# First layer's opening in the form of the second's, set-up products one to a slot, and POOL's second weight split one chunk earlier

## The reference, cut to what matters

```python
# layer 0
mod = silu(condition) @ Wada + bada
sh_a, sc_a, gt_a, sh_m, sc_m, gt_m = split(mod, 6)
xm = layernorm(x, g1, be1) * (1 + sc_a) + sh_a
x = x + gt_a * attention(xm)              # causal
xm = layernorm(x, g2, be2) * (1 + sc_m) + sh_m
x = x + gt_m * (gelu(xm @ W1 + b1) @ W2 + b2)
# layer 1: scale and shift from cond @ w_adaln.T + b, key padding mask, no gates
```

## Time and profile before

| | us |
|---|---|
| median of 3 runs | 1145.15 |
| lowest and highest run | 1138.78, 1145.33 |
| profiled execution | 1142.95 |
| its span | 1141.2 |
| TensorE busy | 1077.1 (94%) |
| DVE busy | 787.0 (69%) |

### The profile page before, as it was taken

How to read it: one execution, slowest core, us unless ns; L and a number is a source line. 1 busy time by engine, 2 the same in 40 slices (tenths; PEclk the granted TensorE clock), 3 DMA queues, 4 the chain that set the end, 5 groups by cost and what they waited for, 6 DMA issues and landing times.

```text
span 1141.2 us, 24601 instructions
## 1 busy us (share of the span) xinstructions
PE 1077.1 (94%) x8972; PEld 943.2 (83%) x8972; DVE 787.0 (69%) x2379; ACT 614.0 (54%) x1239; POOL 262.5 (23%) x269
## 2 busy tenths in 40 slices
PE   3869999999999998999998999999999988999998
PEld 3768898988987687899887788888888767988997
DVE  5467888888886566655647778787787755566553
ACT  1146666666665634443433777777777764344431
POOL 5111131221323334223411111211112221121111
PEclk9779999999998999999997999999999988999999
DMA  7656877667671010000058649465574400010001
GB/s 217 102 85 101 121 139 124 116 106 129 150 106 19 7 61 10 10 10 11 14 86 121 87 71 172 63 92 80 78 92 61 58 2 1 20 37 20 19 20 37
DMA packets 50832, 81.52 MB, mean 71 GB/s; under 512 B 8916, under 2 KB 23476, under 8 KB 49620
## 3 DMA queue, kind: packets, MB, share of 16 engines
q1 hardware_dynamic: 50232, 79.16, 40.0%
q10 hardware_dynamic: 480, 0.79, 0.6%
HBM read 22.64 MB, written 8.44 MB: 27 GB/s over the span
## 4 chain that ended last, share of the span: by engine, by line
PE 84%; DVE 5%; DMA 4%; issue 2%; ACT 2%; SPq 2%; ACTq 0%; POOL 0%; POOLq 0%; DVEq 0%
PE g_bank L573 15%; PE st_bank L573 14%; PE o_bank L661 9%; PE o_bank L573 8%; PE s_bank L573 8%; PE s_bank L628 6%; PE st_bank L647 5%; PE st_bank L641 4%; PE s_bank L624 3%; PE st_bank L643 3%; PE g_bank L719 2%; DMA k_stack<-qk_split 2%; SPq L430 1%; PE s_bank L771 1%; PE s_bank L625 1%
## 5 line engine op out<-in xcount | busy, mean ns | idle before, releaser
L860 ACT ACTIVATE probs<-st_bank 128x384 f32<-128x384 f32 (+1 forms) x512 | 274.1, 548 | 146.1 <-PE st_bank L643 82.7
L1154 DVE CUSTOM_DVE_ANT_0 s_bank<-s_bank,tri_wide 128x128 f32<-128x128 f32 (+1 forms) x512 | 170.2, 386 | 35.4 <-PE s_bank L625 34.2
L1160 DVE TENSOR_REDUCE maxima<-s_bank 128x2 f32<-128x512 f32 x256 | 168.3, 684 | 27.9 <-PE s_bank L628 27.3
L952 ACT ACTIVATE probs<-st_bank,cols 128x512 f32<-128x512 f32 x112 | 77.1, 689 | 202.3 <-PE st_bank L573 186.8
L573 PE MATMUL st_bank<-qk_split,q_stack 128*128 128x512 f32 x696 | 168.4, 400 | 4.9 <-ACT probs L952 4.0
L573 PEld LDWEIGHTS st_bank<-qk_split,q_stack 128*128 128x128 f32 x696 | 130.4, 190 | 37.7 <-ACT probs L952 5.4
L573 PE MATMUL g_bank<-xmT,wa 128*128 128x256 f32 x768 | 122.3, 299 | 4.8 <-POOL xmT L1355 4.8
L661 PE MATMUL o_bank<-probs,v_sb 128*32 128x256 f32 (+1 forms) x2048 | 125.7, 364 | 0.0
L628 PE MATMUL s_bank<-k_stack,q_stack 97*128 97x256 f32 x512 | 116.1, 312 | 6.5 <-DMA k_stack<-qk_split 2.7
L1355 POOL TENSOR_TENSOR xmT<-xm_full,xmT 128x512 fp32r<-128x512 f32 x32 | 42.3, 1322 | 321.4 <-ACT xmT L926 321.4
L573 PEld LDWEIGHTS g_bank<-xmT,wa 128*128 128x128 f32 x768 | 105.1, 200 | 5.8 <-issue 5.2
(11 more groups left out here) (121 smaller groups left out, 2143.4 us busy)
## 6 DMA issues: line engine op xcount, KB each, us to landing
q_stack<-qk_split SPq DMA_DIRECT2D x192, 128.0 KB, 4.6
k_stack<-qk_split SPq DMA_DIRECT2D x186, 128.0 KB, 6.1
gate_rows<-gate_dram SPq DMA_DIRECT2D x32, 128.0 KB, 3.4
w_dram<-w_in SPq DMA_DIRECT2D x8, 512.0 KB, 7.1
wm_f32r<-w_dram SPq DMA_DIRECT2D x4, 1024.0 KB, 10.1
out<-x_sb SPq DMA_DIRECT2D x8, 512.0 KB, 2.9
x_sb<-x_in SPq DMA_DIRECT2D x4, 512.0 KB, 7.0
q_stack<-q_stack SPq DMA_DIRECT2D x4, 384.0 KB
```

The costliest lines, as they stand in the source:

```text
L860: activation(probs[:, h % 8, 0:n], st_bank[h % 2][:, 0:n], ACT.Exp, scale=SCALE)\
L952: activation(h_of[b.const > 0][:, m % 2], h_bank(b, m)[:, :], ACT.Gelu, bias=cols[:, cb + m:cb + m + 1]).then_inc(m_gelu, 1)
L1154: last = v.tensor_tensor_reduce(out=bank[:, keys], in0=bank[:, keys], in1=tri_wide[:, T - (i + 1) * P:T], scale=1.0, scalar=LOWEST, op0=AL ...
L1160: v.reduce_max(maxima[:, gb.mod(2), :, slot], bank[:].rearrange("p (i n) -> p i n", n=T), AX.X).then_inc(max_done, 1)
```

## The change

Five things move.

1. The calls ahead of layer 0's loop are now new(0), project(0), new(1), project(1), on PE and ACT, and the loop starts at step 2 without a projection of q and k, as in layer 1. The v projection of batch 1 stays in slots 6 and 7 of step 2 (`v_due`). On DVE only project(0) stands ahead of the loop; its low parts of batch 1 stay in step 2 among the maxima of batch 0. The six DMAs of k for batch 1 are issued by ACT as those of batch 0 are.
2. `set_up(s)` replaces `set_up_columns` and `set_up_rows` on PE: slots 0 to 11 hold one pair of L539's instructions each, slots 12 and 13 two row instructions each, slot 14 the two for the bias. It writes to o_bank instead of s_bank. It is called for layer 0 in any `step` whose t is AHEAD, and that is so for two calls: `step(0, Step(2), "project")` ahead of the loop, and step 2 in the loop.
3. DVE's part of the set-up stands behind step 2 instead of ahead of it.
4. SyncE's `store_tables` and `load_gates` stand behind the two restacks of a step instead of ahead of them; `load_x(2)` stands behind the restack of q of batch 1.
5. POOL's split of the second attention weights stands in `mlp_step` 2, behind the deviation of chunk 2, instead of in `mlp_step` 3. The memset of the ones columns in v_sb is in two parts.

```diff
+        def v_due(layer, t, only):
+            if layer == 0 and t.const == AHEAD:
+                return only is None
+            return active(layer, t, only)[1].within(B)
...
-            if layer == 1 and t.const == AHEAD:
+            if t.const == AHEAD:
                 return n, off, b, c, d
...
-                    if layer == 0:
-                        when(x_added, c.count(1, -1))
-                        load_gates(c, 0)
...
+                if layer == 0 and c.within(B):
+                    if c.const == 0:
+                        store_tables()
+                    when(x_added, c.count(1, -1))
+                    load_gates(c, 0)
...
+            def set_up(s):
+
+                if s == 0:
+                    pe.wait_ge(late_loaded, 16 * LATE_LOADS)
+                if s < 2 * NF:
+                    last = columns(o_bank, s, ada0, COLUMN_PARTS[2] * D + s * P, silu)
+                elif s < 6 * NF:
+                    last = columns(o_bank, s, ada1, (s - 2 * NF) * P, cond)
...
+                    if layer == 0 and t.const == AHEAD:
+                        set_up(s)
...
+            step(0, Step(0), "new")
+            pe.wait_ge(setup_done, 1)
+            step(0, Step(1), "project")
+            step(0, Step(1), "new")
+            step(0, Step(2), "project")
             for layer in range(LAYERS):
-                for t in steps(B, AHEAD * layer, 5):
...
+                for t in steps(B, AHEAD, 5):
                     step(layer, t)
-                    if layer == 0 and t.const == 1:
-                        set_up_columns()
-                        set_up_rows()
...
-                    if s == SLOT["k"][1] and a.within(B) and a.const + layer == 0:
+                    if s == SLOT["k"][1] and a.within(B) and layer == 0 and a.const < 2:
                         act.wait_ge(k_lo, ga.count(1, 1))
...
+                if layer == 0 and t.const == AHEAD:
+                    a = t - 1
...
-                if layer == 0 and t.const == 3:
+                if layer == 0 and t.const == 2:
                     for f in range(NF):
                         pool.wait_ge(wa_high, 2 + f)
```

More of the change, by code:

```diff
@@ L701, in step @@
                                 last.then_inc(ready, 1)
-                    if s in SLOT["v"] and a.within(B):
+                    if s in SLOT["v"] and v_due(layer, t, only):
                         i = SLOT["v"].index(s)
+                        ga = in_layer(layer, t - 1)
                         if i == 0:
@@ L993, in mlp_step @@
                     step(1, Step(2), "project")
+            step(0, Step(0), "new")
+            step(0, Step(1), "project")
+            step(0, Step(1), "new")
+            step(0, Step(2), "project")
             for layer in range(LAYERS):
-                for t in steps(B, AHEAD * layer, 5):
+                for t in steps(B, AHEAD, 5):
                     if t.const == 3:
-                        act.wait_ge(setup_done, 3)
-                        act.wait_ge(mask_stored, 16)
                         wait(act, m_added, 2 * NCH * layer or None)
@@ L1303, in _ @@
             for layer in range(LAYERS):
-                for t in steps(B, layer + 1, 5):
-                    if layer == 0 and t.const == 1:
-                        split_attention_weights()
+                if layer == 0:
+                    split_attention_weights()
+                    row_statistics(0, Step(1))
+                    row_normalise(0, Step(1))
+                    step(0, Step(1), "project")
+                    set_up_constants()
+                for t in steps(B, AHEAD, 5):
                     step(layer, t)
-                    if layer == 0 and t.const == 1:
+                    if layer == 0 and t.const == AHEAD:
                         set_up_columns()
@@ L1356, in modulated_low, with step @@
                     .then_inc(xmT_ready, 1)
-            def step(layer, t):
-                n, d = t, t - 4
+            def step(layer, t, only=None):
+                n, a, b, c, d = active(layer, t, only)
                 gd = in_layer(layer, d)
@@ L1407, in mlp_step @@
                         row_deviation(1, Step(1))
+            step(0, Step(0), "new")
+            row_deviation(0, Step(1))
+            g_.memset(v_sb[:, 0:2, :, :, HD:32], 1.0).then_inc(vones_set, 1)
+            modulated_low(0, Step(1))
+            g_.memset(q_stack[:, 2].bitcast(fp32), 0.0).then_inc(stack_set[2], 1)
             for layer in range(LAYERS):
-                for t in steps(B, AHEAD * layer, 5):
+                for t in steps(B, AHEAD, 5):
                     step(layer, t)
-                    if layer == 0 and t.const == 0:
-                        g_.memset(q_stack[:, 2].bitcast(fp32), 0.0).then_inc(stack_set[2], 1)
-                    if layer == 0 and t.const == 1:
+                    if layer == 0 and t.const == AHEAD:
                         pool.wait_ge(mods_ready, 2)
-                        g_.memset(v_sb[:, :, :, :, HD:32], 1.0).then_inc(vones_set, 1)
+                        g_.memset(v_sb[:, 2:VBUFS, :, :, HD:32], 1.0).then_inc(vones_set, 1)
                 for t in steps(NCH, 1, 2):
```

67 lines of the change are left out of this document (33 added, 34 removed).

## The result

The changed kernel takes 1148.31 us in the median of 19 runs (1143.26 to 1152.26), the kernel before 1144.11 us in the median of 19 beside them (1138.17 to 1147.31). The ratio is 1.0041, 95% interval 1.0025 to 1.0058. The change makes the kernel 4.2 us slower; the forecast had 1142.5 us, 1.6 us under the median of before. The changed kernel's profiled execution took 1150.0 us, its span is 1148.2.

The account below looks back on a forecast made before the run. TensorE, busy 1077.1 of 1141.2 us, was taken as the bound. The profiled 1142.95 plus 3.5 for the opening minus 5.1 for the split made 1141.35; 1142.5 was given, between that and 1143.55, with range 1136 to 1151.

Parts of the forecast that it names:

- T2: Start of batch 0's scores on TensorE: 44.28 us before the change, forecast at 47.9, 3.6 later.
- 4.2 for the projection and 10.3 for the set-up: TensorE's work from 33.4 us to the scores of batch 0, between bounds of 3.1 + 7.2 and 5.3 + 14.5.
- low-clock rival: Opening at 1.2 GHz throughout: batch 0's scores at 53.2, batch 1's at 76.3, total 1152 us; chance 0.18.
- T3: Start of batch 1's scores on TensorE: 63.14 us before the change, forecast at 66.7, 3.5 later.
- its own sign: Forecast wrong if batch 1's scores start before 62 or after 71, the chunk stays above 25, or later steps give back.
- From T2 to T3: Step 2: 18.8 us by DVE and the DMAs, 17.8 by TensorE (bounds 12.4 to 23.1), both ending together.
- 11.1 us of before: From DVE's low part of k of batch 1 to batch 1's scores, through k's six DMAs; taken as unchanged.
- The hole ahead of the projection: TensorE idle from 30.0 to 33.4 us, as batch 1's projection waits for POOL's low part.
- The split: POOL's weight split in layer 0's MLP: costs nothing in its new place, saves 5.1 us, could be 1.8.
- DVE's part of the set-up: Columns and rows between batch 0 and batch 1, mostly covered by DVE's idle time; 0 to 1 us uncovered.
- The gate load's move: Behind the restacks, 128 KB less ahead of q's and k's DMAs; the 2.44 us wait may shrink by up to 1.0.
- The reading of the clock rule: Read on busy share, fully busy set-up products should get the high clock; the earlier trace disagreed with 0.50.

Follow-up runs that it names:

- e4: The changed kernel with POOL's split of the second attention weights back in `mlp_step` 3; 1153.25 us, ratio 1.0086 to the kernel before.
- e2: The changed kernel with the set-up products issued once, ahead of the loop only; 1150.66 us, ratio 1.0064 to the kernel before.
- e6: e1 with 18 of 24 set-up column instructions moved into TensorE's idle stretches ahead of the loop; 1134.27 us, ratio 0.9921 to the kernel before.
- e3: The kernel before with only POOL's split of the second attention weights moved to `mlp_step` 2; 1139.27 us, ratio 0.9964 to the kernel before.
- e9: e1 with `store_tables` and `load_gates` put back ahead of the restacks; 1137.28 us, ratio 0.9955 to the kernel before.
- e1: The changed kernel with the set-up products issued once, in step 2 of the loop; 1136.28 us, ratio 0.9930 to the kernel before.
- e10: The kernel before with its block of set-up products issued twice; 1154.90 us, ratio 1.0118 to the kernel before.
- e5: e1 with ACT's copy of v of batch 0 ahead of its six DMA issues; 1138.68 us, ratio 0.9948 to the kernel before.
- e8: The changed kernel with the first set-up copy's 24 column instructions 256 columns wide; 1147.30 us, ratio 1.0033 to the kernel before.

## Why the prediction was wrong

**The step that failed is the size of T2.** The mechanism was named: the set-up products are issued twice, the first copy in the open. Its price was not right. The forecast took "4.2 for the projection and 10.3 for the set-up", since "Projection products mixed in should raise the clock after the first slots". Measured from one group's start to the next, the projection took 5.7 us and the set-up 14.8, together 20.5 from 33.54 to 54.00, all of it at a clock of 0.50. (The 5.30 us for 24 projection products, read as the slow price, come from a stretch whose granted clock reads 1.00, 17.95 to 23.09; at 0.50 they take 5.7.) That is the low-clock rival's 5.3 + 14.5 to within 0.7 us, and its T2 of 53.2 and T3 of 76.3 stand against 54.00 and 76.06. The earlier trace rows had the evidence: 0.50 under set-up products that kept TensorE fully busy. The middle of two bounds was chosen without a row that showed a rise under such a mixture. e4's profile shows that the rise can come at 38, so the course is possible; 0.55 for it against 0.18 for the low clock was too much. Why the clock rose in one execution and not in the other stays open. The forecast had set its own sign, that it is wrong if T3 is later than 71.

**From T2 to T3.** The forecast had 18.8 us by DVE and the DMAs and 12.4 to 23.1 by TensorE, with both ending together. Measured are 22.1, by TensorE, near the low clock's bound. This is the second half of the same error, 3.3 us. The other path was mis-sized too, though it did not decide here: e2 and e6, where the DMAs do set T3, have 20.6 and 20.5 us. The term is the "11.1 us of before" for the DMAs, which took 13.4 in both. The forecast had put at nothing that "the load of x in front of them in the one case and beside them in the other" changes them. In e2 that load is issued at 59.29, just ahead of k's issues at 60.01, where the kernel before issues it at 46.22. No run moves that load alone, so this is the likely reason and not a shown one; in e3, with the old order, the leg took 8.5 us. So no run bears out 18.8 us for the new form, and without any set-up in step 2 T3 would still have come at 73 to 75.

**The hole ahead of the projection** was right: forecast 33.4, measured 33.54.

**The split** was right in its size (5.1 forecast, 5.03 in the chunk) and in its mechanism: the addition beside it was not held. In the medians it is 4.2 and 4.9 us. The trace and e3 and e4 bear out the exclusive pair of ports that the Trainium skill tells of ("SBUF — State Buffer", section "SBUF: two separate sides"): 2.62 and 2.71 us beside POOL, 0.42 and 0.69 alone, and no hold where one input is PSUM.

**What was set at nothing.** DVE's part of the set-up behind step 2 brought a wait of 1.65 us at 80.57, where 0 to 1 had been put. The gate load's move gave 0.7 us in the profiles (e9), so the two nearly cancel, as written, with up to 1 us left over.

**What the forecast left out** is the value of the form itself, with one copy: it was never priced apart. e1 and e3 have the same split and one copy each, and differ in the form of the opening. e1's ratio is 0.0034 lower, 3.0 us in the medians. The two intervals overlap a little (0.9948 to 0.9957), so the gain is likely, not shown; all six executions of e1 lie under e3's median. With it the sum closes: -0.0036 for the split (e3), -0.0034 for the form (e1 against e3) and +0.0111 for the first copy (the changed kernel against e1) make +0.0041, the ratio that was measured. The closing is by construction; what checks it are e4 (split, 4.9 us) and e10 (copy, 13.3 us), which measure two of the terms again in the other form.

In the profiled executions the steps add up too: 1142.95 + 12.9 (T3) - 5.0 (the split) = 1150.9, and 1150.0 was measured. That it closes to 0.9 us is luck in part: 2.3 us of the shift at T3 are gone before the chunk, and 1.5 come on in layer 1.

**The reading of the clock rule.** The Trainium skill, "TensorE: Matmul & The Clock Gate", section "Part 1: The HAM clock gate", read on the busy share, would have the high clock in 34 to 54. The row has 0.50 there at a busy share of 1.00, as the earlier trace rows had before; e4 has 1.00 from 38 to 42 at the same busy share. That rule, read so, does not forecast this kernel's opening.

## What to carry to other kernels

When a helper moves from a place in the program into a function that is called in more than one mode, count its instructions in the order: one missing condition (`only is None`) cost 12 us here and turned a gain of 7 into a loss of 4. Price work in the open at the clock that rows of the same kind of work show; where two levels are possible, forecast from the level that was seen, and keep the other for the range. And before work is taken out of a stretch, ask what else ends there: e2 emptied half of step 2 and gained nothing, e5 turned idle time into a wait for the DMAs. A distance that one trace shows for a set of DMAs holds for the transfers that stood beside them there; it was 8.5, 11.1 and 13.4 us here.

## What the runs showed of the hardware

- In plain fp32, 28 records of 16 columns take 5.99 us at a clock of 0.50 and 3.19 at 1.00 (e4), and 28 records of 256 columns 6.21 at 1.00 (e8). Under the narrow ones the weight loads alone are busy for 1.96 of 2.00 us. So products with a sixteenth of the columns take half the time and not a sixteenth; that the weight loads set this pace is the reading of these rows, not tested.
- A fully busy TensorE kept 1.2 GHz for 20 us (34 to 54) and again for 16 us (58 to 74). Wide row products did not raise it at once: in e10 the clock is 0.50 from 40 to 46, most of it under row and bias products of 256 columns, and 0.93 in the four us after, under products of 16 columns. In e4 it fell under the row products.
- The clock goes with most of the spread of a single kernel: over the 18 executions of the kernel before beside e1 to e4 the mean clock is 0.959 to 0.969, and its correlation with the time is -0.87.
- The same instructions got another clock in another execution: 0.50 from 38 to 42 in the changed kernel, 1.00 in e4. T2 differs by 5.9 us between the two.
- Six DMAs of k landed 2.7 us apart in two executions of the same opening (T3 63.14 and 60.45). A start that waits for a DMA, taken from one profile, has that much play.
